# Key weights through another queue, band scores inside the query projection, tile 0's output later

## The reference

```python
x = x + layernorm(attn(layernorm(x)))
x = x + layernorm(ffn(layernorm(x)))

# attn: q, k, v = h @ Wq.T + bq, h @ Wk.T + bk, h @ Wv.T + bv; blocks of 64 tokens (64 blocks)
# block 0 and block 63:     softmax over all 4096 keys
# block 1:                  keys of blocks 0, 1, 2, 63
# block i = 2..61:          keys of blocks 0, i-1, i, i+1, 63   (the band)
# block 62:                 keys of blocks 0, 61, 62, 63
# ffn: silu(h @ wg.T) * (h @ wu.T), then @ wd.T; the int32 weights are scaled by 1/127; hidden 3072
```

## Time and profile before

| | us |
|---|---|
| median of 3 runs | 1537.91 (1537.34 to 1538.02) |
| the profiled execution | 1537.16 |
| span of its slowest core (core 1) | 1536.1 |
| spans of cores 0 to 7 | 1524.9, 1536.1, 1530.1, 1535.7, 1525.5, 1535.6, 1533.3, 1533.3 |

### The profile page before, as it was taken

One profiled execution on the slowest core, in us unless ns is written; L12 is line 12 of the kernel. 1 busy time (PEld: TensorE's weight loads), 2 busy tenths in 40 slices (PEclk: granted clock), 3 DMA queues, 4 the chain that ended last, 5 costly groups with the idle time before them and its releaser, 6 DMA issues.

```text
span 1536.1 us, 26835 instructions; the slowest of 8 cores (1524.9 to 1536.1 us)
## 1 busy us (share of the span) xinstructions
PE 1496.2 (97%) x10032; PEld 723.2 (47%) x10032; DVE 660.0 (43%) x1264; ACT 452.5 (29%) x587; POOL 262.4 (17%) x576
## 2 busy tenths in 40 slices
PE   3999999999999999999999999999999999999998
PEld 2445555555555544444444444444444444444443
DVE  5164454554634354244344344435424434433113
ACT  2266555555556611111111111111101111111111
POOL 4022232332323531010010010011001001000001
PEclk9999999999999999999999999999999999999999
DMA  9655677878766876323333223423322423312002
GB/s 212 117 106 109 133 139 161 170 158 173 131 129 114 298 253 206 94 90 96 90 117 92 67 97 95 110 83 110 89 77 90 96 90 116 96 49 96 1 1 96
DMA packets 130494, 178.43 MB, mean 116 GB/s; under 512 B 65472, under 2 KB 97216, under 8 KB 128960
## 3 DMA queue, kind: packets, MB, share of 16 engines
q1 hardware_dynamic: 110912, 99.11, 26.3%
q0 software_dynamic: 19024, 77.08, 19.4%
q10 hardware_dynamic: 432, 0.53, 0.2%
HBM read 136.85 MB, written 69.21 MB: 134 GB/s over the span
## 4 chain that ended last, share of the span: by engine, by line
PE 96%; DMA 2%; issue 1%; ACT 1%; DVE 1%; POOL 0%; DVEq 0%; SPq 0%; ACTq 0%; POOLq 0%
PE ps L662 21%; PE ps L652 21%; PE ps L712 21%; PE ps L292 15%; PE ps L322 8%; PE ps L375 4%; PE ps L433 3%; PE ps L429 1%; PE ps L436 1%; DMA xx<-x_in 1%; DMA attn_d<-ast 1%; PE ps L620 1%; DMA xst<-x_in 1%; ACT pb L389 0%; PE ps L262 0%
## 5 line engine op out<-in xcount | busy, mean ns | idle before, releaser
L662 PE MATMUL ps<-x2T,wu_sb 128*128 128x512 bf16 x1536 | 363.7, 380 | 2.9 <-DVE hsw L668 2.9
L652 PE MATMUL ps<-x2T,wg_sb 128*128 128x512 bf16 x1536 | 363.6, 380 | 0.0
L712 PE MATMUL ps<-wd_sb,hsw 128*128 128x512 bf16 x1488 | 322.5, 379 | 0.0
L668 DVE TENSOR_TENSOR hsw<-ps,sgb 128x512 bf16<-128x512 f32 x192 | 132.6, 691 | 313.0 <-PE ps L662 313.0
L666 ACT ACTIVATE sgb<-ps 128x512 bf16<-128x512 f32 x192 | 114.6, 597 | 514.0 <-PE ps L652 498.1
L662 PEld LDWEIGHTS ps<-x2T,wu_sb 128*128 128x128 bf16 x1536 | 150.3, 98 | 184.9 <-issue 4.5
L652 PEld LDWEIGHTS ps<-x2T,wg_sb 128*128 128x128 bf16 x1536 | 150.4, 98 | 181.7 <-issue 1.6
L712 PEld LDWEIGHTS ps<-wd_sb,hsw 128*128 128x128 bf16 x1488 | 145.6, 98 | 175.6
L173 POOL TENSOR_TENSOR small<-small 128x1 f32<-128x1 f32 x127 | 75.5, 594 | 766.8 <-DVE small L171 766.8
L389 ACT ACTIVATE pb<-ps 128x1024 bf16<-128x1024 f32 (+2 forms) x128 | 117.5, 957 | 131.0 <-PE ps L375 131.0
L380 ACT ACTIVATE pb<-ps 128x1024 bf16<-128x1024 f32 x128 | 124.1, 1022 | 49.8 <-PE ps L375 49.8
(11 more groups left out here) (78 smaller groups left out, 1076.8 us busy)
## 6 DMA issues: line engine op xcount, KB each, us to landing
xx<-x_in SPq DMA_DIRECT2D x34, 512.0 KB, 5.5
attn<-attn_d SPq DMA_DIRECT2D x32, 512.0 KB, 3.8
x_d<-xx POOLq DMA_DIRECT2D x32, 512.0 KB, 6.7
x1r<-x_d SPq DMA_DIRECT2D x32, 512.0 KB, 3.4
out<-x1r POOLq DMA_DIRECT2D x31, 512.0 KB, 3.0
xst<-x_in SPq DMA_DIRECT2D x29, 512.0 KB, 6.1
attn_d<-ast SPq DMA_DIRECT2D x58, 256.0 KB, 3.6
wgb_d<-wgT POOLq DMA_DIRECT2D x24, 256.0 KB, 5.1
```

What stands on the lines that cost most here:

```text
L652: mm = te.matmul(gp[:, p2], wg_sb[:, hc * 1024 + dc * 128:hc * 1024 + (dc + 1) * 128], xTn[:, dc * 512:(dc + 1) * 512], start=(dc == 0), s ...
L662: mm = te.matmul(upp[:, p2], wu_sb[:, hc * 1024 + dc * 128:hc * 1024 + (dc + 1) * 128], xTn[:, dc * 512:(dc + 1) * 512], start=(dc == 0), ...
L668: tok["hu", g] = DV.sig(dv.tensor_tensor(hsw[:, hc * 512:(hc + 1) * 512], upp[:, p2], sgb[:, p2], ALU.mult))
L712: mm = te.matmul(ys[:, half * 512:(half + 1) * 512], hsw[:, hc * 512 + tt * 128:hc * 512 + (tt + 1) * 128], wd_sb[:, hc * DM + half * 512: ...
```

## The change

Four edits. First, units 0 to 3 of the keys' weights (the former key loads 0 and 1) are loaded as fp32 into a new buffer `wst` by four DMAs from SP, issued between x tiles 3 and 4, and cast by four ScalarE instructions in turns t = 0..3 of the loop, ahead of `xT_pe(t - 1)`. Second, SP no longer waits for tiles 1 and 2 before it issues the loads of 4 and 5. Third, in chunks 0 and 7 `scores` 2 is issued between the fourth and the fifth matmul of the query group, and `scores` 3 behind the group. Fourth, in the passage the order is gate 0, gate 1, last context, gate 2, up 0, up 1; silu 0 and 1 follow their gates directly, and tile 0's division, store and SP's wait come after `up(3)`.

```diff
+    wst = at("wst", TOP, 4 * 1024, F32)
     for t in range(4):
         x_load(t)
+    d_ws = [Dma(nc, "d_ws%d" % i) for i in range(4)]
+    for u in range(4):
+        tok["wst", u] = d_ws[u].sig(sy.dma_start(wst[:, u * 1024:(u + 1) * 1024], wk_d[u]))
     for t in (4, 5):
-        SY.need(tok["x", t - 3])
         x_load(t)
+    def wk_cast(u):
+        AC.need(tok["wst", u])
+        tok["wk", u] = AC.sig(ac.activation(wk_sb[:, u * 1024:(u + 1) * 1024],
+                                            wst[:, u * 1024:(u + 1) * 1024], AF.Identity))
-    def qk_group(c, u, name, w_sb):
+    def qk_group(c, u, name, w_sb, between=None):
...
         for dc in range(8):
+            if dc == 4 and between is not None:
+                between()
-    w_turn = {0: ((wk_load, 0),), 1: ((wk_load, 1),), 2: ((wk_load, 2),), 3: ((wk_load, 3),),
-              4: ((wv_load, 0),), 5: ((wv_load, 1),), 6: ((wq_load, 0), (wq_load, 1)),
-              7: ((wq_load, 2), (wq_load, 3))}
+    w_turn = {2: ((wk_load, 2),), 3: ((wk_load, 3),), 4: ((wv_load, 0),), 5: ((wv_load, 1),),
+              6: ((wq_load, 0), (wq_load, 1)), 7: ((wq_load, 2), (wq_load, 3))}
...
+        if t < 4:
+            wk_cast(t)
         if t >= 1:
             xT_pe(t - 1)
...
-        if n + 1 < len(slots):
+        if few:
+            q_group(*slots[n + 1], lambda: scores(c, u, 2, 0))
+            scores(c, u, 3, 1)
+        elif n + 1 < len(slots):
             q_group(*slots[n + 1])
-        if few:
-            band_scores()
...
     gate(0)
+    silu(0)
+    gate(1)
+    silu(1)
     pv(7, 7)
-    gate(1)
-    DV.need(tok["g", 7, 7])
-    for i in range(2):
-        tok["gdone"] = to_attn(...)
-    tok["attn", 0] = tuple(tok["as", i] for i in range(3))
+    gate(2)
     up(0)
     up(1)
-    SY.need(*tok["attn", 0])
...
+            if g >= 3:
+                gate(g)
             if g >= 2:
-                gate(g)
                 up(g)
+            if g == 3:
+                tile0_out()
```

More of the change, by code:

```diff
@@ L215, in w_load @@
     def w_load(name, d_w, w_sb, w_d, i):
-        tok[name, i] = d_w[i].sig(po.dma_start(
+        tok[name, 2 * i] = tok[name, 2 * i + 1] = d_w[i].sig(po.dma_start(
             w_sb[:, i * 2048:(i + 1) * 2048].rearrange("p (u e) -> p u e", u=2),
             w_d[2 * i:2 * i + 2].rearrange("u p e -> p u e")))
+    def wk_cast(u):
+        AC.need(tok["wst", u])
+        tok["wk", u] = AC.sig(ac.activation(wk_sb[:, u * 1024:(u + 1) * 1024],
+                                            wst[:, u * 1024:(u + 1) * 1024], AF.Identity))
     def wk_load(i):
@@ L286, in q_buf @@
         return qb[:, o:o + 512]
-    def qk_group(c, u, name, w_sb):
+    def qk_group(c, u, name, w_sb, between=None):
         b, bank = rot_bank()
-        TE.need(tok[name, u // 2], *(tok["xT", 4 * c + j] for j in range(4)))
+        TE.need(tok[name, u], *(tok["xT", 4 * c + j] for j in range(4)))
         for dc in range(8):
+            if dc == 4 and between is not None:
+                between()
             mm = te.matmul(bank, w_sb[:, u * 1024 + dc * 128:u * 1024 + (dc + 1) * 128],
@@ L304, in k_group, with q_group @@
             kt[:, o:o + 512], bank, AF.Identity, bias=bk[:, u:u + 1], scale=1.0))
-    def q_group(c, u):
-        b, bank, t = qk_group(c, u, "wq", wq_sb)
+    def q_group(c, u, between=None):
+        b, bank, t = qk_group(c, u, "wq", wq_sb, between)
         tok["qmm", c] = t
@@ L546, in build_nc @@
         more = c + 1 < NCH
-        def band_scores():
-            scores(c, u, 2, 0)
-            scores(c, u, 3, 1)
         scores(c, u, 0, 0)
         scores(c, u, 1, 1)
-        few = c in (0, NCH - 1) and n + 1 < len(slots)
         if more and c > 0:
             k_group(c + 1, u)
-        if n + 1 < len(slots):
+        few = c in (0, NCH - 1) and n + 1 < len(slots)
+        if few:
+            q_group(*slots[n + 1], lambda: scores(c, u, 2, 0))
+            scores(c, u, 3, 1)
+        elif n + 1 < len(slots):
             q_group(*slots[n + 1])
-        if few:
-            band_scores()
         if n >= 1:
@@ L562, in build_nc @@
         if not few:
-            band_scores()
+            scores(c, u, 2, 0)
+            scores(c, u, 3, 1)
         if more:
@@ L654, in gate, with silu @@
         tok["gate", g] = TE.sig(mm)
+    def silu(g):
+        p2 = slice((g % 2) * 512, (g % 2 + 1) * 512)
+        AC.need(tok["gate", g], tok.get(("hu", g - 2)))
+        tok["sg", g] = AC.sig(ac.activation(sgb[:, p2], gp[:, p2], AF.Silu, scale=DQ))
     def up(g):
@@ L664, in up @@
         tok["gu", n] = t_u = TE.sig(mm)
-        AC.need(tok["gate", g], tok.get(("hu", g - 2)))
-        tok["sg", g] = AC.sig(ac.activation(sgb[:, p2], gp[:, p2], AF.Silu, scale=DQ))
+        if g >= 2:
+            silu(g)
         DV.need(tok["sg", g], t_u)
@@ L672, in build_nc, with tile0_out @@
     gate(0)
+    silu(0)
+    gate(1)
+    silu(1)
     pv(7, 7)
-    gate(1)
-    DV.need(tok["g", 7, 7])
-    for i in range(2):
-        tok["gdone"] = to_attn(1, 8, gacc[:, i * 520:(i + 1) * 520].rearrange(
-            "p (h t e) -> p h t e", t=1, e=65), attn_d[0:128, i * 512:(i + 1) * 512].rearrange(
-            "p (t e) -> p t e", t=1))
-    tok["attn", 0] = tuple(tok["as", i] for i in range(3))
+    gate(2)
     up(0)
     up(1)
-    SY.need(*tok["attn", 0])
     PO.need(tok["s", 7, 7], tok["gu", 0])
+    def tile0_out():
+        for i in range(2):
+            tok["gdone"] = to_attn(1, 8, gacc[:, i * 520:(i + 1) * 520].rearrange(
+                "p (h t e) -> p h t e", t=1, e=65), attn_d[0:128, i * 512:(i + 1) * 512].rearrange(
+                "p (t e) -> p t e", t=1))
+        tok["attn", 0] = tuple(tok["as", i] for i in range(3))
+        SY.need(*tok["attn", 0])
     for n in range(NCH):
```

## The result

The changed kernel takes 1552.7 us (median of 6 runs; the kernel before 1537.97 beside it), ratio 1.0093 [1.0079, 1.0108]: 14 us slower. Forecast was 1548.5, in a range of 1539 to 1554. In one of the runs of each kernel, and in some runs of the experiments, one half of the chip ran at a lower clock; the ratios leave those out and the medians do not.

What follows compares the result with a forecast made beforehand. TensorE, busy for 97% of the span, was taken as the bound. Start 15 + chunk 0 2.8 - chunk 7 1.2 - passage 6.0 = +10.6 us on 1537.16 gives 1547.8; the runs' median lies 0.75 above: 1548.5, range 1539 to 1554.

Steps and rivals of the forecast that it cites:

- Start: Up to the fourth key group: tiles 4 to 7 land later in SP's longer queue, +15 us; ends +5 and +19.5.
- tile 4 lands before 27 us: At the start: a stated sign that the prediction is wrong; it expected tile 4 at about 32.5 us instead of 22.6.
- q1's traffic before q0 joins: SP's queue at the start: 473 packets by 13 us, then 59 a us until GpSimd's queue starts at 18 us.
- The lower of the two readings: At the start: q1 alone at 90 packets a us, fourth key group 13 us late; the other reading gave +17.6 us.
- Chunk 0: Eight slots: 0.2 us of matmul shape changes plus 0.15 us wait for the exponential each, +2.8 us; ends +1 and +4.
- Chunk 7: Seven slots: six gain 0.17 us, the first loses 0.3, the last gains about 0.6; -1.2 us, ends -3 and +0.5.
- the memset that its context waits for is earlier too: Last slot of chunk 7: the reason given for its gain of about 0.6 us.
- Passage: Attention to FFN: context wait 1.2, stall 3.0 and low clock 1.84 us all go; -6.0 us, ends -4.5 and -6.3.
- which hides some 5 us: In the passage: tile 5's loads come late behind tile 0's stores, but use four slots of 3.46 us on hides this.
- rival (d): In the passage: deferred divisions meet stores still out, only 2 us gained; +14.6 in sum, 1552.5 us; chance 0.08.
- Rival (b): At the start: q1 brings nine transfers by 20 us, tile 4 no later; -4.4 in sum, 1533.5 us; chance 0.09.
- (a): At the start: q1 fast, q0 late, value weights harmless; start +5, sum +0.6, 1538.5 us, no change; chance 0.12.

Runs made afterwards that it cites:

- E4: The whole change with the four query loads ahead of the two value halves in GpSimd's queue: 1545.4 us, ratio 1.0039 to the kernel before.
- E1: The kernel before with only the start changed (key units on SP's queue, ScalarE's casts, no SP waits for tiles 1 and 2): 1554.14 us, ratio 1.0111.
- E7: Start as before the change, E6's passage, scores 2 behind the fifth query matmul in chunks 0 and 7: 1537.87 us, ratio 0.9985 to the kernel before.
- E6: E3 without SP's wait for tile 0's stores: 1533.15 us, ratio 0.9954 to the kernel before.
- E10: E9 with E8's chunk 7 (scores 2 behind the fifth query matmul): 1532.31 us, ratio 0.9964 to the kernel before.
- E3: The kernel before with only the passage's new order (fourth edit): 1534.9 us, ratio 0.9969.
- E5: The whole change with the fp32 key weights queued behind tiles 4 and 5, each cast just ahead of its key group: 1561.35 us, ratio 1.012 to the kernel before.
- E9: E6 with the last two tiles' normalisation and transposing DMA one slot earlier in each chunk: 1532.09 us, ratio 0.996 to the kernel before.
- E8: Start and chunk 0 as before, E6's passage, scores 2 behind the fifth query matmul in chunk 7 only: 1536.7 us, ratio 0.996 to the kernel before.

## Why the prediction was right, and where it was off

**Start (+15, measured +14.9 on core 1).** The kind of loss was right: a longer queue, then an equal count of packets with the value halves (338 and 347), a fourth key group late. But the prediction's own sign of being wrong was met: "tile 4 lands before 27 us". It came at 26.34 on core 1 and at 24.0 to 26.4 on seven cores in all, not at 32.5 (on core 6 it came at 32.58, for a reason that was not found). Mis-sized was q1's traffic before q0 joins: 586 packets by 13 us for 473, then 95 a us for 59, so that 1089 were through at 20 us where the sum gives 858. Why q1 was that fast is open. From 20 us on the rates were as taken. The lower of the two readings, "tile 4 would be seen at 29 and tile 7 at 46.6, and the fourth group be 13 us late", is what happened to tile 7 and the group (46.77, 13.5 us); the other 1.4 us is the key group at half speed, which stood in the upper end alone. The +15 lies between the two readings, so that it agrees to 0.1 us is luck in part, and the other cores have 12.1 to 19.8.

On core 6, with tile 4 late, the stretch from the first key group to the first value group was 32.3 us; elsewhere it was 40 to 43: the two delays replace each other. E4 separates them, and E1, with +17 (14 to 20), agrees with the sum. The rule cited from the Trainium skill (DMA: Bandwidth & Descriptors, Queues, rings and completion order), turns between the queues a packet at a time, agrees with the counts; that the size of a neighbour's packets does not change this is what E4 shows, by giving tiles 5 to 7 another neighbour.

**Chunk 0 (+2.8, +2.7).** Both terms are shown: E7 took away the wait and got back 0.15 a slot, and 0.20 stayed, the two changes to 64-row matmuls and back. The Trainium skill (TensorEngine Tiling (Array Packing), Key Properties) states that a change of the tiling mode drains TensorE; a cost at each change agrees with it.

**Chunk 7 (-1.2, -0.6).** The six slots behind the first gained 0.94 together (1.02 forecast), and the first lost 0.36 (0.3). The last slot was to gain 0.6 and gained nothing (3.46 and 3.46). The failed step is "the memset that its context waits for is earlier too": the waits of 0.36 and 0.55 did go, but the context then waits 0.99 for `gacc`. The last slot has no query group between the second scores and `pv(7, 6)`, and VectorE had not yet summed `(7, 5)`.

**Passage (-6.0, -4.1).** The wait of the last context, the stall and the low clock behind it went as worked out. Mis-sized was "which hides some 5 us": SP's wait for tile 0's stores and tile 5's load took 8.92 + 9.30 us, and `up` started 1.8 us late, nearly all of the 1.9 that are missing. E6 takes SP's wait away. The divisions did not meet stores that were still out, as rival (d) has it; that the time, 1552.7, is (d)'s 1552.5 is chance.

**The rest.** On core 1 the steps add to +12.6 for a forecast of +10.6. The prediction was worked out for core 1 alone, and the time is that of the slowest of eight. The other 3.1 us of the profiled execution come from no step of the change that the trace shows: core 6 set the end, through one late transposing DMA of tile input in its chain,

```profile
303.95 0.82 DVE xn L177
...
305.23 16.87 DMA xT<-xn
```

where the median is 6.8 us; its slot took 13.74 us instead of 7.7. Its start alone would not have made it the slowest (first value group 4.8 us ahead of core 1's). The kernel before had one too, on core 5 (15.77, chunks 1 to 6 3.4 us longer), a core whose start was 3.6 us ahead of core 1's, so it did not set the end. Rival (b), a start that loses under 4.4 us, is out by E1, although its tile 4 under 27 us came true; (a) is out by tile 7's time.

## What to carry over

Moving a load from one queue to another changes not only what is ahead in the new queue but what the other queue reaches meanwhile: list for every tile both its place and its neighbour, and put long rows behind whatever is still needed. When a wait is removed, look for what the same engine is queued behind next (here the accumulation, and SP's wait in front of the next loads), and leave a blocking wait out of a queue that also issues loads. A split of a group costs its shape changes (0.2 us here) in every repetition, so it has to remove a wait longer than that.

## What was not expected of the hardware

With q0 still empty, q1 moved 95 packets a us (13 to 16 us, core 1), where it had moved 63 from 4 to 8 us. GpSimd issued a load at 12.24 and the first packets of q0 came after 16 us. The transposing DMA from SP has a long tail: 5 to 9 us in a core's median, but in each of the 12 profiled executions one core or two, in E10 four, saw a landing of 15.8 us or more (E1 17.70, E3 17.63, E5 17.83, E9 20.6, E10 22.6), most often in chunk 3; in the old order of issue it cost that core 2 to 8 us. Its cause was not found. TensorE stopped without a releaser for 1 to 2.8 us in late slots of chunk 7 or just behind them, where the FFN's weights are loaded: on two to five cores of each kernel with edit 3 or a variant of it (on cores 5 and 7 of the change), on at most one of E1, E3, E6 and E9, and for under 1 us on one of the kernel before. In E7, E8 and E10 that took back what the shorter slots gave; the trace names no releaser, and the cause stays open.
